# Mamba-style layer with experts on eight cores: float32 moments in the norm, a delayed convolution, and state-space decay tables prepared for a whole chunk

## The reference, cut to what matters

```python
xn = layernorm(x)                                  # no weight, no bias
z  = xn @ W_in                                     # 2048 x-columns, 1024 B, 1024 C, 16 dt
xs = silu(causal_conv(z_x, taps=4) + conv_b)       # depthwise
delta = softplus(dt + delta_param); a = exp(-delta * abs(dt))
h_t = a_t * h_{t-1} + x_t b_t^T                    # 16 heads, state 128 x 64
y_t = h_t c_t
y = sigmoid(xn @ W_gate) * y
y = y * rsqrt(mean(y*y) + eps) * norm_w
attn = y @ W_out
ffn  = top-1 of 8 experts: (silu(xn @ w1a) * (xn @ w1g)) @ w2, times its probability
out  = x + attn + ffn
```

## Time and profile before

| | us |
|---|---|
| two timed runs | 8437.13 and 8949.89 |
| their median, the time before | 8693.51 |
| the profiled execution, its own time | 8084.42 |
| its span (slowest core, core 5) | 8082.8 |
| spans of the eight cores | 8037.5 to 8082.8 |
| TensorE busy in that span | 6564.4 |
| VectorE busy | 3218.3 |
| ScalarE busy | 1677.6 |

### The profile page before, as it was taken

How to read it: one execution, slowest core, us unless ns; L and a number is a source line. 1 busy time by engine, 2 the same in 40 slices (tenths; PEclk the granted TensorE clock), 3 DMA queues, 4 the chain that set the end, 5 groups by cost and what they waited for, 6 DMA issues and landing times.

```text
span 8082.8 us, 90722 instructions; the slowest of 8 cores (8037.5 to 8082.8 us)
## 1 busy us (share of the span) xinstructions
PE 6564.4 (81%) x28776; PEld 2841.2 (35%) x28776; DVE 3218.3 (40%) x6706; ACT 1677.6 (21%) x1615; POOL 41.3 (1%) x82
## 2 busy tenths in 40 slices
PE   3546459899998999999835464599999999999998
PEld 1212124344443444444312121244444444344443
DVE  4353443434334343433343534434333343434333
ACT  2212213122121312112122122121221313122120
POOL 0000000000000000000000000000000000000000
PEclk7759569999999999999967595799999999999999
DMA  2304024444444444444422040244444444444443
GB/s 80 99 11 149 29 73 140 145 135 149 136 150 130 148 144 134 153 130 157 128 88 94 11 157 21 82 138 148 131 156 131 155 131 141 146 134 153 133 154 123
DMA packets 407431, 979.74 MB, mean 121 GB/s; under 512 B 46048, under 2 KB 308480, under 8 KB 337344
## 3 DMA queue, kind: packets, MB, share of 16 engines
q1 hardware_dynamic: 400896, 956.48, 36.2%
q0 software_dynamic: 6080, 17.46, 0.7%
HBM read 965.10 MB, written 8.39 MB: 120 GB/s over the span
## 4 chain that ended last, share of the span: by engine, by line
PE 72%; DVE 11%; issue 6%; DMA 5%; ACT 3%; DVEq 2%; ACTq 1%; POOL 0%; SPq 0%; POOLq 0%
PE p_fa L1142 21%; PE p_fg L1152 21%; PE p_fo L1244 19%; DVE acc L1305 2%; PE p_w L939 2%; PE p_sb L630 2%; DVE tmp L1301 2%; PE p_z L411 2%; PE p_z L335 1%; DMA stg<-w1t 1%; DMA stg<-wgate 1%; DMA stgw<-w2t 1%; ACT L659 1%; PE pY L787 1%; PE p_cv L358 1%
## 5 line engine op out<-in xcount | busy, mean ns | idle before, releaser
L1244 PE MATMUL p_fo<-A,w2bf 128*128 128x512 bf16 x8192 | 1876.7, 393 | 276.3 <-DVE w2bf L1211 276.2
L1142 PE MATMUL p_fa<-xn,wbf 128*128 128x512 bf16 x8192 | 1856.7, 380 | 27.2 <-DVE wbf L1127 23.9
L1152 PE MATMUL p_fg<-xn,wbf 128*128 128x512 bf16 x8192 | 1852.2, 379 | 0.0
L1164 ACT ACT_TABLE_LOAD x512 | 656.9, 1283 | 4418.8 <-PE p_fa L1142 4418.8
L1097 DVE TENSOR_TENSOR A<-wbf,p_fg 128x1024 bf16<-128x1024 bf16 x512 | 625.0, 1221 | 2145.4 <-PE p_fg L1152 2145.4
L1244 PEld LDWEIGHTS p_fo<-A,w2bf 128*128 128x128 bf16 x8192 | 821.5, 101 | 1329.2 <-issue 447.3
L1142 PEld LDWEIGHTS p_fa<-xn,wbf 128*128 128x128 bf16 x8192 | 801.1, 98 | 1002.8 <-issue 46.5
L1152 PEld LDWEIGHTS p_fg<-xn,wbf 128*128 128x128 bf16 x8192 | 801.6, 98 | 966.9 <-issue 1.4
L1211 DVE CAST w2bf<-stgw 128x256 bf16<-128x256 f32 x2048 | 587.9, 293 | 1167.9 <-PE p_fo L1244 848.8
L1127 DVE CAST wbf<-stg 128x2048 bf16<-128x2048 f32 x484 | 593.7, 1227 | 51.6 <-DVE A L1097 2.7
L1164 ACT ACTIVATE wbf<-p_fa 128x1024 bf16<-128x1024 f32 x512 | 524.4, 1024 | 5.7
(11 more groups left out here) (145 smaller groups left out, 2476.6 us busy)
## 6 DMA issues: line engine op xcount, KB each, us to landing
stg<-w1t SPq DMA_DIRECT2D x512, 1024.0 KB, 4.8
stgw<-w2t SPq DMA_DIRECT2D x2048, 128.0 KB, 2.2
stg<-win_x SPq DMA_DIRECT2D x64, 768.0 KB, 5.0
stg<-wgate SPq DMA_DIRECT2D x64, 512.0 KB, 4.3
stg<-wout SPq DMA_DIRECT2D x32, 1024.0 KB, 5.3
stg<-win_b SPq DMA_DIRECT2D x32, 512.0 KB, 3.9
stg<-win_c SPq DMA_DIRECT2D x32, 512.0 KB, 3.5
acc<-u_t POOLq DMA_DIRECT2D x16, 512.0 KB, 10.8
```

The lines of the kernel that those rows point to most:

```text
L1142: ins = t.matmul(p_fa[p][:, tsl * 512:(tsl + 1) * 512], wbf[:, p * 2048 + k * 128: p * 2048 + (k + 1) * 128], xn[:, k * HT + tsl * 512: k ...
L1152: ins = t.matmul(p_fg[p][:, tsl * 512:(tsl + 1) * 512], wbf[:, p * 2048 + 1024 + k * 128: p * 2048 + 1024 + (k + 1) * 128], xn[:, k * HT + ...
L1164: ins = s.activation(wbf[:, p * 2048: p * 2048 + 1024], p_fa[p][:, :], AF.Silu)
L1244: ins = t.matmul(p_fo[gp_par * 4 + o2 * 2 + tsl][:, :], w2bf[:, s4 * 256 + o2 * 128: s4 * 256 + (o2 + 1) * 128], A1[:, j * HT + tsl * 512: ...
```

## The change

Three edits.

- Norm: the cast to `ubf` is gone. The float32 `acc` itself is the moving operand of the first sum, the squares are written as float32 to `tmp1024`, and both sums are float32 matmuls with the last column of the float32 triangle `tri01` (all ones). The squares have one buffer: the square of chunk c waits until both matmuls of chunk c-1 are done.
- z: `x_pre` has two buffers, and the convolution and the Silu of block m-1 are issued after the main matmuls of block m.
- State space: `Dbf`, `expSB`, `alph` get two buffers by chunk parity, `t_e` becomes bfloat16 with two buffers by group. The preparation of all four groups of a chunk (`emit_prep`) is issued in one go: for chunk 0 ahead of its first head, for chunk kq+1 behind head 7 of chunk kq. The exponential of `Dbf` leaves the preparation and becomes a section of its own, issued ahead of the first head of its group.

```diff
-        t_e = sb("t_e", [128, 512], F32)
+        t_e = sb("t_e", [128, 1024], BF16)
...
                 def f_v(v):
...
-                        if cch >= 2:
-                            v.wait_ge(sems["pe"], pe_base + (cch - 2) + 1)
-                        v.tensor_copy(ubf[:, p * 512:(p + 1) * 512], sl)
-                        ins = v.tensor_tensor(usq[:, p * 512:(p + 1) * 512], sl, sl,
+                        if cch >= 1:
+                            v.wait_ge(sems["pe"], pe_base + cch)
+                        ins = v.tensor_tensor(tmp1024[:, 0:QT], sl, sl,
                                               op=ALU.mult)
...
-                        t.matmul(p_s1[:, :], onescol[:, :], ubf[:, p * 512:(p + 1) * 512],
+                        t.wait_ge(sems["ve"], sq_v[cch])
+                        t.matmul(p_s1[:, :], tri01[:, 127:128], sl,
                                  start=(cch == 0), stop=(cch == NKC - 1))
-                        ins = t.matmul(p_s2[:, :], onescol[:, :],
-                                       usq[:, p * 512:(p + 1) * 512],
+                        ins = t.matmul(p_s2[:, :], tri01[:, 127:128],
+                                       tmp1024[:, 0:QT],
                                        start=(cch == 0), stop=(cch == NKC - 1))
...
                     def f_v(v, m=m, p=p):
+                        xo = p * (QT + 3)
                         v.wait_ge(sems["pe"], mm_pe[m])
+                        if m >= 2:
+                            v.wait_ge(sems["pe"], cv_pe[m - 2])
...
+                    if m >= 1:
+                        emit_conv(m - 1)
+                    if m == NIC - 1:
+                        emit_conv(m)
...
+                def emit_prep(kq, gd):
...
                         def f_t4(t, qq=qq, dg_f=dg_f, gd=dict(gd)):
                             t.wait_ge(sems["dG"], dg_f)
                             if qq >= 1:
+                                t.wait_ge(sems["ve"], st["sb_ve"][qq - 1])
+                                t.wait_ge(sems["ac"], st["sb_ac"][qq - 1])
...
                             s.drain()
-                            ins = s.activation(t_e[:, :],
-                                               Dbf[:, qq * 512:(qq + 1) * 512],
+                            ins = s.activation(alph[:, par * 16 + qq * 4:
+                                                    par * 16 + (qq + 1) * 4],
...
+                            st["sb_ac"].append(inc(ins, "ac"))
...
+                        if hh == 0:
+                            def f_se(s, kq=kq, qq=qq, par=par, gb=gb):
+                                s.wait_ge(sems["ve"], st["sb_ve"][qq])
+                                s.wait_ge(sems["ve"],
+                                          te_mp_marks.get(gb - 2, mps[1]))
+                                ins = s.activation(
+                                    t_e[:, (gb % 2) * 512:(gb % 2 + 1) * 512],
...
+                                    AF.Exp, bias=cc[0:128, 3:4], scale=-1.0)
+                                e_marks[gb] = inc(ins, "ac")
+                            sect("scalar", f_se)
...
+                        if h == 7 and kq + 1 < QT // Q:
...
+                            emit_prep(kq + 1, g2)
```

More of the change, by code:

```diff
@@ L67, in build_program @@
         w2bf = sb("w2bf", [128, 1024], BF16)
-        x_pre = sb("x_pre", [128, QT + 3], BF16)
+        x_pre = sb("x_pre", [128, 2 * (QT + 3)], BF16)
         tails = sb("tails", [128, NIC * 3], BF16)
-        Dbf = sb("Dbf", [128, NH * Q], BF16)
-        expSB = sb("expSB", [128, NH * Q], BF16)
-        alph = sb("alph", [128, 16], F32)
+        Dbf = sb("Dbf", [128, 2 * NH * Q], BF16)
+        expSB = sb("expSB", [128, 2 * NH * Q], BF16)
+        alph = sb("alph", [128, 32], F32)
         dtw = sb("dtw", [128, 4 * 64], F32)
@@ L364, in z_phase, with emit_conv, f_t2, f_s2 @@
-                    sect("tensor", f_t2)
-                    def f_s2(s, m=m, p=p):
-                        s.wait_ge(sems["pe"], cv_pe[m])
-                        ins = s.activation(A1[:, 24 * HT + m * QT: 24 * HT + (m + 1) * QT],
-                                           p_cv[p][:, :],
-                                           AF.Silu, bias=convb[:, m:m + 1])
-                        silu_a.append(inc(ins, "ac"))
-                        note("scalar", ins)
-                    sect("scalar", f_s2)
+                    def emit_conv(mc):
+                        pc = mc % 2
+                        def f_t2(t, mc=mc, pc=pc):
+                            xo = pc * (QT + 3)
+                            t.wait_ge(sems["ve"], evac_v[mc])
+                            if mc >= 2:
+                                t.wait_ge(sems["ac"], silu_a[mc - 2])
+                            ins = None
+                            for kk in range(DC):
+                                ins = t.matmul(p_cv[pc][:, :],
+                                               wbf[:, pc * 2048 + 1024 + kk * 128:
+                                                   pc * 2048 + 1024 + (kk + 1) * 128],
+                                               x_pre[:, xo + kk:xo + kk + QT],
+                                               start=(kk == 0), stop=(kk == DC - 1))
+                            cv_pe.append(inc(ins, "pe"))
+                        sect("tensor", f_t2)
+                        def f_s2(s, mc=mc, pc=pc):
+                            s.wait_ge(sems["pe"], cv_pe[mc])
+                            ins = s.activation(
+                                A1[:, 24 * HT + mc * QT: 24 * HT + (mc + 1) * QT],
+                                p_cv[pc][:, :], AF.Silu, bias=convb[:, mc:mc + 1])
+                            silu_a.append(inc(ins, "ac"))
+                            note("scalar", ins)
+                        sect("scalar", f_s2)
@@ L601, in ssd_phase @@
                 state["ssd_prev_d4"] = ve_d4q
-                e_ac_prev_chunk = state["ssd_prev_ac"]
                 pv_xtok = ve_d4q
@@ L607, in ssd_phase, with f_g @@
                 ve_wb = ve_d4q
-                prev_mp_last = ve_d4q
-                prev_pe_sb = C["pe"]
                 hist_mp = [ve_d4q, ve_d4q]
                 hist_yg = [ve_d1, ve_d2]
-                for kq in range(QT // Q):
-                    pe_sb, sb_ve, sb_ac = [], [], []
-                    mp_hist = []
-                    def f_g(g, kq=kq, prev_pe_sb=prev_pe_sb):
+                prep_st = {}
+                te_mp_marks = {}
+                ygs = state["ssd_yg_slot"]
+                mps = state["ssd_mp_slot"]
+                ess = state["ssd_e_slot"]
+                def emit_prep(kq, gd):
+                    st = {"pe_sb": [], "sb_ve": [], "sb_ac": []}
+                    prep_st[kq] = st
+                    par = kq % 2
+                    def f_g(g, kq=kq, gd=dict(gd)):
                         g.wait_ge(sems["ve"], ve_d2)
-                        g.wait_ge(sems["pe"], prev_pe_sb)
+                        g.wait_ge(sems["pe"], gd["prev_pe_sb"])
                         inc(g.dma_start(
@@ L662, in f_s2 @@
                             s.drain()
-                            if qq >= 1:
-                                s.wait_ge(sems["ve"], mp_hist[-1])
-                            else:
-                                s.wait_ge(sems["ve"], prev_mp_last)
-                            s.activation(alph[:, qq * 4:(qq + 1) * 4],
-                                         alph[:, qq * 4:(qq + 1) * 4], AF.Exp,
-                                         bias=cc[0:128, 3:4], scale=-1.0)
-                            s.drain()
@@ L823, in ssd_phase @@
                     state["ssd_prev_yg"] = max(hist_yg)
+                    state["ssd_prep_last"] = prep_st[kq]
                 state["ssd_prev_ac"] = C["ac"]
```

367 lines of the change are left out of this document (194 added, 173 removed).

## The result

| | before | changed |
|---|---|---|
| runs | 10 | 12 |
| median, us | 8418.83 | 8459.62 |
| lowest and highest | 8072.75 to 8949.89 | 8193.48 to 9125.43 |
| ratio | | 1.0104, 95% interval 1.0055 to 1.0154 |

A forecast was written before the change was run, and what follows sets the result against it. It took the stages touched to be bound by chains of waits between engines, the experts' matmuls being untouched. Terms of 0 (z), 67 (norm) and 32 (state space) gave +99 us on 8084, times 1.075 8800 us, range 8330 to 9070.

The forecast's parts named there:

- the carry-over to the timed scale: Whole kernel: the sum in the profiled execution's microseconds is multiplied by 8693.51/8084.42 = 1.075, giving 8800 us.
- within 2%: Whole kernel: the changed time can't be told from no change, on the slow side; chance 0.77.
- the sign: Whole kernel: the change makes it slower, by 99 us on 8084, +1.2%.
- Norm, forecast +67: Norm's moments: serial chunks with float32 matmuls, two at half clock and six at full, +16.8 us a phase, +67 in four.
- The rival that the norm stays at half clock: Norm: all eight chunks at half clock, +111 us, with state space +143, 1.8% slower; chance 0.12.
- State space, forecast +32: State-space phase: preparations stay one chain and new sections load tables, +8.0 us a phase, +32 in four.
- The Trainium skill's rule: State space: exponentials in a row need no table load, so +12 us in place of +32, total +79; chance 0.06.
- z, forecast 0: z phase: the delayed convolution is done 0.16 us before the cast wants it, so a block stays at 4.22 us.
- The clock rival: z phase: TensorE's clock falls to 1.2 GHz, 6.6 us a block, +144 us, in all +243, 3.0% slower; chance 0.12.
- The hidden preparations: State space: preparations hide behind heads, a group 8.3 us in place of 14.2, total 7773, -3.8%; chance 0.07.

The follow-up runs named there:

- e11: The changed kernel without an edit, run once more beside the kernel before; no ratio, lowest 8194.87 us.
- e1: The changed kernel with the old norm (bfloat16 cast, squares and sums, two buffers); ratio 1.0054 to the kernel before, lowest 8111.08 us.
- e5: The changed kernel with two buffers for the norm's float32 squares; ratio 1.0133 to the kernel before, lowest 8188.15 us.
- e2: The changed kernel with the old state-space phase and its old buffers; ratio 1.0098 to the kernel before, lowest 8151.76 us.
- e4: The changed kernel with the first following head's Dbf exponential moved into the preparation's fourth ScalarE section; ratio 1.0125 to the kernel before, lowest 8170.05 us.
- e3: The changed kernel with the old z phase and one x_pre; ratio 1.0146 to the kernel before, lowest 8186.62 us.
- e9: The changed kernel with z's main weights' cast ahead of the copies on VectorE; ratio 1.0084 to the kernel before, lowest 8144.07 us.
- e6: The changed kernel with each group's preparation issued one group ahead, between heads; no ratio, lowest 8002.45 us.
- e8: The changed kernel with old norm, old z and preparation one group ahead, its broadcast in four pieces; ratio 0.9725 to the kernel before.

## Why the prediction was wrong

The comparison with the kernel before came out as forecast, and the microseconds did not. Point by point:

**The step that failed is the carry-over to the timed scale.** "I work the sum in the profiled execution's microseconds and carry it over by 8693.51/8084.42 = 1.075", to 8800 us. The median of 8693.51 came from two runs. Ten runs have a median of 8418.83 and begin at 8072.75, beside the profiled execution. In that execution's own scale the sum was 8183 us, and the lowest six of the twelve runs of the changed kernel lie at 8193.48 to 8206.36. The measured median of 8459.62 is 340 us below the 8800, inside the 8330 to 9070, a range whose width is the runs' own scatter and says little of the change. The factor was the mis-sized term: over ten runs it is 8418.83/8084.42 = 1.041, not 1.075, which would have given 8521, and the changed kernel's median is 1.034 times the sum of 8183. Neither says anything of the change: such a factor only tells how a kernel's runs scatter above one of them. Taken against 8418.83 the 8800 would be +4.5%, four times the measured +1.0%. The chance of 0.77 for "within 2%", and the sign, were right.

**Norm, forecast +67, measured +63.** The four phases of core 5 took 25.97, 25.91, 25.96 and 24.28 us in place of 9.82, 9.68, 9.92 and 9.26: +63.4. In three of them two chunks at half clock took 4.52 each (4.68 forecast) and six 2.82 (2.85); in the fourth only one was at half clock. The rival that the norm stays at half clock did not come: the granted clock was 0.50 from 90 to 98 us and 0.97 behind it. The forecast had no term for the experts' phases, which are longer by some 6 to 7 us each with this norm (e11). e1 undoes the term, e5 parts it in two.

**State space, forecast +32, measured +32.4.** The four phases of core 5, from the first broadcast to the first square of the norm behind them, took 240.27, 239.68, 239.47 and 240.67 us in place of 232.42, 232.08, 231.63 and 231.54: +8.1 each (8.0 forecast). Link 6.15 (6.18), last link 8.95 (8.90), heads as before. e2 and e4 show this term and the table load in it. The Trainium skill's rule ("ScalarE: Activation LUTs", section "Table sets: the hidden batching unit") would have made this term +12: with 128 loads for exponentials alone the trace goes against it, and e4, which only moves one exponential into another section, gains 18 us.

**z, forecast 0, measured +4.8.** The four phases of core 5, from the first cast to the first cast for B, grew by 0.4, 0.6, 1.8 and 2.0 us; the lowest times of e3 and the changed kernel differ by 7. The order was right (the cast stands in VectorE's row, and the convolution is done when the cast wants it), but the copies' start was taken as fixed at 2.00 us and it is 2.06 with matmuls queued behind. The clock rival did not come: 4.28 us a block is full clock. e9 shows that it is the cast behind the copies that kept the move from paying.

**The hidden preparations, 0.07.** Not so in the changed kernel, for the reason given: four broadcasts in a row. e6 and e8 show what that rival described when the order does place heads between them, though at 10.1 to 11.4 us a group and not 8.3, since TensorE's and VectorE's own parts of the preparation stay on the heads' chain. That is the step of that rival that was too kind.

The terms measured in the phases sum to 63.4 + 32.4 + 4.8 = 100.6 us on 8084, +1.24%, against 99 forecast. That all three came so close, and that the errors of norm and z cancel, is in part luck: the norm moves by 1.7 us with each chunk that is at half clock or not, from phase to phase and core to core.

## What to carry to other kernels

Issuing work earlier on in-order engines hides nothing by itself: ask what stands between two links of the chain on each engine's own row. Here four links in a row only moved a stall, and the same links laid between the users of the group before (e8) took 2.7% off. A second buffer pays only where the next wait in the row isn't late at the same time: the delayed convolution needed the cast moved too (e9). A precision change that removes a cheap cast must be priced by the longer matmuls and by the single buffer that replace it. And a sum made in one execution's scale is not to be multiplied onto a median of two scattered runs.

## What the runs showed of the hardware

- A float32 matmul of 512 columns with 128 rows and one weight column costs TensorE 0.86 us at full clock and 1.66 at half (starts 50.86 to 51.72 and 39.01 to 40.67), the bfloat16 one 0.21 at full (82.91 to 83.12 in the earlier trace rows): four times.
- The first activation of each ScalarE section of this program is preceded by a 1283 ns table load even if the section before it used the same function: 64 loads for L680 and 64 for L717, exponentials alone. An exponential added to a section that had its load has none (e4, 384.20).
- A matmul group's end reached VectorE 0.06 us later when other matmuls stood right behind it (2.06 against 2.00 us, in every regular block; back to 2.00 and 4.22 in e3). What makes it was not looked into.
- The granted clock can leave its full level in the middle of dense matmuls, and on some cores only: in e8 it was 0.81 on cores 0 to 5 between 1060 and 1210 us, and 1.00 on cores 6 and 7, with TensorE busy throughout on all of them.
